# Twelve small tables copied into one and gathered jointly for the first two groups; dense features turned first; chunk 0 stored batch by batch

## The reference

```python
e = stack([tbl_f[ids[:, f]] for f in range(32)], axis=1)      # 512 x 32 x 64
# layer 0, then layer 1, with hidden = e at first
z = einsum('bhd,bfd->bhfd', hidden, e).reshape(B, -1, D)
y = relu(einsum('bcd,oc->bod', z, w) + b[None, :, None])      # 128 outputs
# layer 0: hidden = y[:, :64], direct = y[:, 64:]; layer 1: direct = y
z = concat(directs, axis=1).sum(-1)                           # 512 x 192
h = relu(concat([z, dense_ctx], 1) @ W_top1 + b_top1)
y = relu(h @ W_top2 + b_top2) @ W_top3
```

## Time and profile before

| | us |
|---|---|
| median of 3 runs | 1061.82 |
| lowest, highest | 1060.72, 1062.32 |
| the profiled execution | 1062.44 |
| its span | 1060.6 |

### The profile page before, as it was taken

How to read it: one execution, slowest core, us unless ns; L and a number is a source line. 1 busy time by engine, 2 the same in 40 slices (tenths; PEclk the granted TensorE clock), 3 DMA queues, 4 the chain that set the end, 5 groups by cost and what they waited for, 6 DMA issues and landing times.

```text
span 1060.6 us, 11306 instructions
## 1 busy us (share of the span) xinstructions
PE 1017.3 (96%) x3519; PEld 661.0 (62%) x3519; DVE 947.4 (89%) x777; ACT 770.0 (73%) x908; POOL 917.9 (87%) x310
## 2 busy tenths in 40 slices
PE   2399999999999999999999999999999999999999
PEld 1146566566666666666666666666766666666663
DVE  3089999999999999999999999999999999999991
ACT  5047666677878877877778777877787887788772
POOL 6528888799999999999999999999988989899880
PEclk9999999999999999999999999999999999999999
DMA  6498888878878877888778878887776776777630
GB/s 173 96 223 195 186 186 193 183 180 193 190 174 191 187 185 179 191 194 189 176 182 193 187 175 192 193 191 170 168 169 167 171 183 162 166 181 180 161 80 0
DMA packets 140638, 183.92 MB, mean 173 GB/s; under 512 B 55633, under 2 KB 56273, under 8 KB 140450
## 3 DMA queue, kind: packets, MB, share of 16 engines
q1 hardware_dynamic: 135986, 178.93, 72.0%
q0 software_dynamic: 4096, 4.20, 2.7%
q10 hardware_dynamic: 496, 0.06, 0.0%
HBM read 174.66 MB, written 8.39 MB: 173 GB/s over the span
## 4 chain that ended last, share of the span: by engine, by line
PE 64%; DVE 16%; issue 9%; ACT 4%; DMA 2%; ACTq 2%; SPq 1%; POOL 1%; POOLq 0%; DVEq 0%
PE py L723 28%; DVE zf L622 11%; PE py L743 11%; PE py L731 10%; PE py L732 10%; DVE zlB L642 2%; DMA xs<-x_dram 1%; ACTq L502 1%; DVE pzS L631 1%; ACT hid L470 1%; DVE zS L635 1%; ACT hid L469 1%; PE py L762 1%; POOL zl L380 1%; DMA xs<-in_L_rec_w 1%
## 5 line engine op out<-in xcount | busy, mean ns | idle before, releaser
L380 POOL TENSOR_TENSOR zl<-zf,zh 128x2048 fp32r<-128x2048 f32 x178 | 785.5, 4419 | 85.0 <-ACT zh L445 82.5
L622 DVE TENSOR_TENSOR zf<-xs,hid 128x2048 f32<-128x2048 f32 (+1 forms) x256 | 538.6, 2108 | 31.3 <-ACT hid L470 25.6
L723 PE MATMUL py<-zf,wf 128*128 128x512 f32 x944 | 426.9, 592 | 1.2 <-DVE zf L622 1.2
L445 ACT ACTIVATE zh<-zf 128x1536 fp32r<-128x1536 f32 (+1 forms) x184 | 338.2, 1838 | 94.5 <-DVE zf L622 90.5
L731 PE MATMUL py<-zh,wh 128*128 128x512 f32 x736 | 290.5, 395 | 1.5 <-ACT zh L445 1.1
L723 PEld LDWEIGHTS py<-zf,wf 128*128 128x128 f32 x944 | 178.4, 189 | 176.7 <-issue 161.5
L732 PE MATMUL py<-zh,wl 128*128 128x512 f32 x736 | 288.4, 392 | 0.0
L743 PE MATMUL py<-zl,wh 128*128 128x512 f32 x736 | 227.3, 431 | 1.4 <-POOL zl L380 1.4
L743 PEld LDWEIGHTS py<-zl,wh 128*128 128x128 f32 x736 | 138.7, 189 | 66.8 <-issue 36.8
L731 PEld LDWEIGHTS py<-zh,wh 128*128 128x128 f32 x736 | 138.4, 188 | 39.5 <-issue 8.5
L369 POOL DMA_INDIRECT emb<-in_tbl,idx x128 | 132.2, 1033 | 28.8 <-issue 22.6
(11 more groups left out here) (100 smaller groups left out, 608.8 us busy)
## 6 DMA issues: line engine op xcount, KB each, us to landing
xs<-x_dram SPq DMA_DIRECT2D x512, 256.0 KB
xs<-x_dram SPq DMA_DIRECT2D x504, 64.0 KB
x_dram<-emb SPq DMA_DIRECT2D x66, 64.0 KB, 5.6
x_dram<-emb SPq DMA_DIRECT2D x22, 96.0 KB
emb<-in_tbl,idx POOLq DMA_INDIRECT x128
x_dram<-emb SPq DMA_DIRECT2D x4, 384.0 KB
xs<-in_L_rec_w SPq DMA_DIRECT2D x2, 512.0 KB
xs<-in_L_rec_w SPq DMA_DIRECT2D x1, 1024.0 KB
```

Of the source, the lines that this page charges most:

```text
L380: pool.tensor_tensor(zl[:, q, first:T], zf[:, s, first:T], zh[:, q, first:T].bitcast(F32), ALU.subtract).then_inc(lo["P"], 1)
L445: act.activation(zh[:, q, first:T], zf[:, s, first:T], ACT.Copy).then_inc(hi, 1)
L622: dve.tensor_tensor(zf[:, slot(u), first:T], left[:, first:T], view(right, at, [[0, T - first], [1, N]]), ALU.mult).then_inc(mult, 1)
L723: mm = pe.matmul(y, wf[:, w, h], zf[:, s, h], start=first and h == first_tile, stop=ends and h == T - 1)
```

## The change

- `FIRST_BATCHES` is (fields 0-11), (12-16), (17-19), and, as the last, the twelve fields 20-31 (`REST`).
- SyncE copies tables 20 to 31 one after another into one DRAM table `table_joint`, with one transfer for each, after the weights; it loads the ids of the 8 samples of groups 0 and 1 for these fields into `ids_joint`, 96 partitions (12 fields x 8 samples) by 2. DVE builds the first row of each table in the joint one (memsets, times the identity, summed over columns, cast) and adds it to the ids.
- POOL, after the 20 single gathers, waits for the twelve copies and gathers group 0's and then group 1's 96 rows in one transfer each (`gather_joint`). The twelve fields of `REST` are gathered after these.
- SyncE puts group 0's 96 rows into `x32` with one transfer and stores them twice into `x_dram`, and group 1's twice. `load_xd(0)` waits for the stores of fields 0-19 and of joint group 0, `load_x0(1)` for joint group 1. The other 112 samples of `REST` are stored after `load_xe(0)`, and `load_x0(2)` waits for that.
- ScalarE issues eight `x32` transfers for the first batch, five for the second, two for the third; SyncE one for field 19.
- The dense features are loaded after the weights and turned by TensorE ahead of the weights; DVE copies them earlier. The top-layer weights are loaded at g == 50 (`load_top`) instead of at the start.
- One warm-up matmul fewer ahead of the spreading.

The diff, without its context lines:

```diff
@@ -55,12 +55,18 @@
-FIRST_BATCHES = [(0, 0, 12), (0, 12, 12), (0, 24, 5), (0, 29, 3)]
+JOINT = 20
+NJ = F - JOINT
+JOINT_GROUPS = 2
+FIRST_BATCHES = [(0, 0, 12), (0, 12, 5), (0, 17, 3), (0, JOINT, NJ)]
+REST = len(FIRST_BATCHES) - 1
-STORES = [sum(min(m, REPEATS) for b, _, m in BATCHES if b == c) for c in range(NC)]
+STORES = [sum(min(m, REPEATS) for n, (b, _, m) in enumerate(BATCHES) if b == c and n != REST) for c in range(NC)]
@@ -131,6 +137,13 @@
+        ids_joint = sb("ids_joint", [P, JOINT_GROUPS], I32)
+        idx_joint = sb("idx_joint", [P, JOINT_GROUPS], I32)
+        first_row = sb("first_row", [P, NS * NJ])
+        first_rows = sb("first_rows", [P, 1])
+        first_rows_int = sb("first_rows_int", [P, 1], I32)
+        emb_joint = sb("emb_joint", [P, JOINT_GROUPS, D])
@@ -204,7 +217,14 @@
-        ids_in, consts_in, top_in = sem("ids_in"), sem("consts_in"), sem("top_in")
+        offsets = [sum(t.shape[0] for t in tables[JOINT:JOINT + j]) for j in range(NJ + 1)]
+        table_joint = nc.dram_tensor("table_joint", [offsets[NJ], D], F32, kind="Internal")
+        ids_in, consts_in, top_in, dense_in = sem("ids_in"), sem("consts_in"), sem("top_in"), sem("dense_in")
+        ids_joint_in, tables_joined, rows_set, idx_joint_ready = sem("ids_joint_in"), sem("tables_joined"), sem("rows_set"), sem("idx_joint_ready")
+        joint_gathered = [sem("joint_gathered%d" % k) for k in range(JOINT_GROUPS)]
+        joint_stored = [sem("joint_stored%d" % k) for k in range(JOINT_GROUPS)]
+        rest_stored = sem("rest_stored")
@@ -254,25 +274,41 @@
+            sp.dma_start(dense[:], dense_ctx.rearrange("(c p) n -> p c n", p=P)).then_inc(dense_in, 16)
+            for k in range(JOINT_GROUPS):
+                first = ids[NS * k:NS * k + 1, JOINT:JOINT + 1]
+                sp.dma_start(ids_joint[0:NS * NJ, k:k + 1], bass.AP(tensor=first.tensor, offset=first.offset, ap=[[1, NJ], [F, NS], [1, 1]]),
+                             allow_slow_non_contiguous=True).then_inc(ids_joint_in, 16)
-            sp.dma_start(wt1a[H:P, :], W_top1[0:H, :]).then_inc(top_in, 16)
-            sp.dma_start(wt1b[:], W_top1[H:H + P, :]).then_inc(top_in, 16)
-            sp.dma_start(wt2[:], W_top2.rearrange("(k p) n -> p k n", p=P)).then_inc(top_in, 16)
-            sp.dma_start(wt3[:], W_top3.rearrange("(k p) n -> p (k n)", p=P), allow_slow_non_contiguous=True).then_inc(top_in, 16)
-            sp.dma_start(bt1[:], b_top1.rearrange("(k p) -> p k", p=P), allow_slow_non_contiguous=True).then_inc(top_in, 16)
-            sp.dma_start(bt2[:], b_top2.rearrange("(k p) -> p k", p=P), allow_slow_non_contiguous=True).then_inc(top_in, 16)
-            sp.dma_start(dense[:], dense_ctx.rearrange("(c p) n -> p c n", p=P)).then_inc(top_in, 16)
-            sp.wait_ge(cleared, 2)
-            sp.dma_start(wt1a[0:16, :], W_top1[H + P:H + P + 16, :]).then_inc(top_in, 16)
+            for j in range(NJ):
+                sp.dma_start(table_joint[offsets[j]:offsets[j + 1], :], tables[JOINT + j]).then_inc(tables_joined, 16)
+            def load_top():
+                sp.dma_start(wt1a[H:P, :], W_top1[0:H, :]).then_inc(top_in, 16)
+                sp.dma_start(wt1b[:], W_top1[H:H + P, :]).then_inc(top_in, 16)
+                sp.dma_start(wt2[:], W_top2.rearrange("(k p) n -> p k n", p=P)).then_inc(top_in, 16)
+                sp.dma_start(wt3[:], W_top3.rearrange("(k p) n -> p (k n)", p=P), allow_slow_non_contiguous=True).then_inc(top_in, 16)
+                sp.dma_start(bt1[:], b_top1.rearrange("(k p) -> p k", p=P), allow_slow_non_contiguous=True).then_inc(top_in, 16)
+                sp.dma_start(bt2[:], b_top2.rearrange("(k p) -> p k", p=P), allow_slow_non_contiguous=True).then_inc(top_in, 16)
+                sp.wait_ge(cleared, 2)
+                sp.dma_start(wt1a[0:16, :], W_top1[H + P:H + P + 16, :]).then_inc(top_in, 16)
-                if n == 3:
+                if n == REST:
+                    others = NS * JOINT_GROUPS
+                    for i in range(REPEATS):
+                        dst = x_dram[c, i * F + f:i * F + f + 1, D * others:D * others + 1]
+                        sp.dma_start(bass.AP(tensor=dst.tensor, offset=dst.offset, ap=[[D, P - others], [P * D, m], [1, D]]),
+                                     emb[others:P, c % 2, f:f + m, :]).then_inc(rest_stored, 16)
+                    return
+                if n == 2:
-                    load_x32(sp, 31, x32_last)
+                    load_x32(sp, f + m - 1, x32_last)
@@ -284,6 +320,13 @@
+            def store_joint(k):
+                sp.wait_ge(joint_gathered[k], 16)
+                if k == 0:
+                    sp.dma_start(x32[JOINT:F, :], emb_joint[0:NS * NJ, 0]).then_inc(x32_last, 16)
+                for i in range(REPEATS):
+                    sp.dma_start(x_dram[0, i * F + JOINT:i * F + F, N * k:N * k + N], emb_joint[0:NS * NJ, k]).then_inc(joint_stored[k], 16)
@@ -323,18 +366,26 @@
-            for n in range(len(FIRST_BATCHES)):
+            for n in range(REST):
+            store_joint(0)
+            store_joint(1)
+            sp.wait_ge(joint_stored[0], 16 * REPEATS)
+            sp.wait_ge(joint_stored[1], 16 * REPEATS)
+            store_batch(REST)
+            sp.wait_ge(rest_stored, 16 * REPEATS)
+                if g == 50:
+                    load_top()
@@ -363,6 +414,8 @@
+                    if c == 2:
+                        pool.wait_ge(rest_stored, 16 * REPEATS)
@@ -379,7 +432,19 @@
+            def gather_joint(k):
+                if k == 0:
+                    pool.wait_ge(idx_joint_ready, 1)
+                    pool.wait_ge(tables_joined, 16 * NJ)
+                pool.indirect_dma_start(
+                    out=emb_joint[0:NS * NJ, k, :], out_offset=None, in_=table_joint[:],
+                    in_offset=bass.IndirectOffsetOnAxis(ap=idx_joint[0:NS * NJ, k:k + 1], axis=0),
+                ).then_inc(joint_gathered[k], 16)
+                if n == REST:
+                    for k in range(JOINT_GROUPS):
+                        gather_joint(k)
@@ -495,17 +560,19 @@
-            for n in range(2):
-                _, f, m = FIRST_BATCHES[n]
-                act.wait_ge(gathered[n], gathered_count(n))
-                for b in range(NS):
-                    act.dma_start(x32[f:f + m, D * b:D * b + D], emb[b:b + 1, 0, f:f + m, :]).then_inc(x32_in, 16)
+            _, f, m = FIRST_BATCHES[0]
+            act.wait_ge(gathered[0], gathered_count(0))
+            for b in range(NS):
+                act.dma_start(x32[f:f + m, D * b:D * b + D], emb[b:b + 1, 0, f:f + m, :]).then_inc(x32_in, 16)
+            _, f, m = FIRST_BATCHES[1]
+            act.wait_ge(gathered[1], gathered_count(1))
+            for i in range(m):
+                load_x32(act, f + i, x32_in)
+            _, f, m = FIRST_BATCHES[2]
-            for f in range(24, 29):
-                load_x32(act, f, x32_in)
-            act.wait_ge(gathered[3], gathered_count(3))
-            for f in range(29, 31):
-                load_x32(act, f, x32_last)
+            for i in range(m - 1):
+                load_x32(act, f + i, x32_last)
@@ -537,6 +604,7 @@
+            act.wait_ge(top_in, 16 * 7)
@@ -565,6 +633,23 @@
+            for j in range(NJ):
+                dve.memset(first_row[:, NS * j:NS * j + NS], float(offsets[j])).then_inc(rows_set, 1)
+            dve.wait_ge(eye_in, 16)
+            dve.wait_ge(rows_set, NJ)
+            dve.tensor_tensor(first_row[0:NS * NJ], first_row[0:NS * NJ], ident[0:NS * NJ, 0:NS * NJ], ALU.mult).then_inc(rows_set, 1)
+            dve.wait_ge(rows_set, NJ + 1)
+            dve.tensor_reduce(first_rows[0:NS * NJ], first_row[0:NS * NJ], AX_X, ALU.add).then_inc(rows_set, 1)
+            dve.wait_ge(rows_set, NJ + 2)
+            dve.tensor_copy(first_rows_int[0:NS * NJ], first_rows[0:NS * NJ]).then_inc(rows_set, 1)
+            dve.wait_ge(rows_set, NJ + 3)
+            dve.wait_ge(ids_joint_in, 16 * JOINT_GROUPS)
+            dve.tensor_tensor(idx_joint[0:NS * NJ], ids_joint[0:NS * NJ], first_rows_int[0:NS * NJ].to_broadcast([NS * NJ, JOINT_GROUPS]),
+                              ALU.add).then_inc(idx_joint_ready, 1)
+            dve.wait_ge(dense_turned, 1)
+            dve.wait_ge(cleared, 2)
+            dve.tensor_copy(zd[0:16], px0[0:16]).then_inc(s_low, 1)
@@ -580,9 +665,6 @@
-            dve.wait_ge(dense_turned, 1)
-            dve.wait_ge(cleared, 2)
-            dve.tensor_copy(zd[0:16], px0[0:16]).then_inc(s_low, 1)
@@ -684,6 +766,10 @@
+            pe.wait_ge(dense_in, 16)
+            for c in range(NC):
+                tr = pe.transpose(px0[0:16, P * c:P * c + P], dense[:, c, :], ident[:])
+            tr.then_inc(dense_turned, 1)
@@ -693,10 +779,6 @@
-            pe.wait_ge(top_in, 16 * 8)
-            for c in range(NC):
-                tr = pe.transpose(px0[0:16, P * c:P * c + P], dense[:, c, :], ident[:])
-            tr.then_inc(dense_turned, 1)
@@ -777,9 +859,9 @@
-            warm_up(4, py1[:])
```

(6 more changed lines are left out.)

## The result

| | us | ratio to before, 95% interval |
|---|---|---|
| before, 20 runs beside it | 1061.76 | |
| after, 20 runs | 1064.44 | 1.0025, 1.0017 to 1.0032 |
| after again, in the fifth comparison below | 1065.42 | 1.0023, 1.0013 to 1.0034 |
| after again, in the sixth | 1057.63 | 0.9954, 0.994 to 0.9967 |

The change was slower by 0.25%, 2.7 us, where 7.3 less was forecast. The last row is no misprint: the same kernel was faster by 0.46% in another comparison, while the median of the kernel before lay between 1061.6 and 1062.7 in all. Most of this document is about finding why. The profiled execution of the result took 1063.91, with a span of 1062.1, against 1060.6.

What follows compares the result with a forecast made beforehand. TensorE bounds the long middle, a queue of 32 gathers the start. Spreading -14.1, tail +6.3, top weights +0.5 sum to -7.3 us: 1054.5 from 1061.82, its own range 1051.5 to 1057.5, whole range 1047.5 to 1062.0.

Steps and rivals of the forecast that it cites:

- Gain at the spreading: 14.1 us: At the start, the first real matmul (spreading of x32) would move from 48.76 to 34.7, a gain of 14.1 us.
- Copies in time: Before the joint gather: twelve table copies, 3.65 MB, would end at 20.6 to 28.9, before the gather's slot at 29.36.
- The rival that made it slower by waiting for the copies: At the start, POOL stands still until the copies end; at 108 GB/s +8 us, 1069.5; chance 0.14.
- the 10 of 16 engines: Table copies going row by row would use 10 of 16 DMA engines: 67 GB/s and 1085 or more.
- a copied byte count twice: In the table copies, each byte counting twice against HBM gives 179 GB/s, ending near 31, costing some 2 us.
- Crowding: Rival at the start: copies at 196 GB/s make the joint gather 3.1 late; 1057.6, up to 1061; chance 0.20.
- its second door: Crowding's other form at the start: batch 0's x32 transfers and stores stand behind the copies; no separate size.
- One of the signs of being wrong: At the start: ScalarE's small x32 transfers ending after SyncE's joint one would show the forecast wrong.
- Spreading to A(0): Start of chunk 0: steps after the spreading were taken to keep the old trace's distances, 11.06 us here.
- the 0.8 that I had put down as late: At the start of chunk 0, load_xd(0) would start 13.3 us earlier, 0.8 us late against compute.
- Tail of chunk 0: REST stores delay load_x0(2), landing at 64.3, holding up B(0) on TensorE: cost 6.3 us, range 3.5 to 8.
- Top weights at group 50: Seven transfers moved to group 50, issued in 4 us of SyncE idleness: cost 0.5 us, range 0 to 3.

Runs made afterwards that it cites:

- fifth comparison: Unedited rerun of the changed kernel (1065.42, ratio 1.0023), beside the kernel before (1061.48), the changed kernel with x32 read back (1064.84) and another version (1061.02).
- sixth: Unedited rerun of the changed kernel, 1057.63, ratio 0.9954, beside the unedited held version, 1058.76, ratio 0.9968.
- second comparison: Includes the changed kernel with POOL held before the twelve later gathers until the six spreading matmuls were counted: 1064.34.
- the fourth: Four kernels: four joint groups with POOL held (1058.20) or not (1060.74); kernel before with dense first and late top weights (1062.43), or a POOL pause (1065.60).
- held version: Changed kernel with four joint groups, POOL held before REST until the spreading was counted, REST stored at g == 1, seven warm-ups: 1058.20, ratio 0.9966.
- lean one: Held version with REST stored at the end of group 0, joint groups 2 and 3 stored later, top weights over seven groups: 1061.02, ratio 0.9983.

## Why the prediction was wrong

**The step that failed** is the unwritten one between "Gain at the spreading: 14.1 us" and the time at which the gain arrives. The sum took for granted that what follows the spreading moves with it, by the distances of the trace of before. In the result's comparison it didn't: from the spreading to DVE's first product it took 13.5 us (38.20 to 51.74) against 4.6. The spreading was 10.6 early and the first product 1.6; the second product (55.15 against about 54.0) and A(0) (62.08 against 59.82) were late. Before was profiled under the same condition, and its rows mostly hide it: the stores and transfers among the gathers were not urgent, and what was urgent came after the last gather of the burst (45.58). A distance read where nothing hurries can't show what a hand-over costs there. Two things did show it and were passed over: the four issues at 49.06 took 4.09 us, the same four at 849.02 took 1.85; and of the 4.6 us that were carried over from the old trace, ScalarE's copy alone stood 3.7 behind the start of the spreading, against 1.1 in the sixth comparison.

**What lies behind it is open.** Shown is: in four of six comparisons some 1.5 releases a microsecond are recorded while the gathers run and for 5 to 8 us after the last one begins, in all kernels; counts that TensorE raises in that stretch reach the others late, and SyncE's issues are slow; holding POOL ends it early (dense records from 35.75 and the first product at 41.89, second comparison); the two others have none of it. Not shown is what makes it: something of the chip's state, or the recording itself, which would be slowing what it records. The lost records speak for the second, as they go with the lateness comparison by comparison, but they can be its consequence as well, and every execution here was recorded, the timed ones at least by their span. It isn't the chip by its number, as the same number had both. So the kernel's worth on a machine is one of two, 1.0025 and 0.9954, and the runs don't say how often each.

**Point by point**, with the result's comparison first and the sixth second:

- *Copies in time.* Right in both. Their pieces ran from 9.2 to 21.5 and from 9.4 to 21.9, 12.3 us for 3.65 MB or 296 GB/s in the first, near the fast end of what I had drawn (11 to 19.4 us with the gathers beside). The rival that made it slower by waiting for the copies is out, and with it the 10 of 16 engines: the Trainium skill ("DMA: Bandwidth & Descriptors", "Why a DMA increments its semaphore by 16 and not by 1") gives 10 for 1250 rows, but the trace has each table as 16 pieces of 20,000 bytes (16,000 for 1000 rows), with up to 16 of them in flight at once. Nor did a copied byte count twice against the 358 GB/s that the Trainium skill gives in the section "Bandwidth" of that page: twice 296 would be 592.
- *Crowding.* This rival did occur, through its second door, batch 0 behind the copies. Its stores began at 22.40 and 22.80, against 20.55: the rows of its last gather were in at 21.5 and 21.8, against 20.2, behind the pieces of the copies. ScalarE's small transfers took 0.75 and 0.72 each, not 0.67, and in the result's run they also began 1.5 us later than in the sixth comparison (24.31 against 22.86), behind a ScalarE instruction that waited 1.73 us there. So the spreading began at 38.20 and 36.87, not at 34.7: 3.5 and 2.2 short. One of the signs of being wrong came with it: ScalarE's small transfers ended after the joint one (36.28 against 33.82, and 34.83 against 33.97), so ScalarE's chain set the spreading and not SyncE's.
- *Spreading to A(0).* 11.06 in the trace of before and in the forecast; 23.9, and 12.0. In the sixth `x0(1)` had to be waited for (3.30), the 0.8 that I had put down as late.
- *Tail of chunk 0.* SyncE waited for the `REST` stores in both, 6.1 and 5.1 us, and `x0(2)` was copied at 69.60 and at 63.07, forecast 64.3. In the first it hid behind the lateness: B(0) came 16.0 after A(0), as before (16.2). In the sixth TensorE reached B(0) at 66.80, 9.2 early (forecast 68.2, 7.8 early), and not after 6 us of idleness; but the loads behind `x0(2)` were late too, DVE waited 3.70 for them until 71.88, where I had looked only as far as B(0), and from the eighth of ScalarE's copies of `x0` on the lead is about 5.5. So the tail took 10.9 - 5.5 = 5.4 us of the lead at A(0), forecast 6.3. Size right, place half right.
- *Top weights at group 50.* Mis-sized: 0.5 forecast. In the sixth:

```profile
820.47 1.17 SPq L288 DMA_DIRECT2D wt1a<-in_W_top  x1
...
826.56 0.56 SPq L296 DMA_DIRECT2D wt1a<-in_W_top  x1
```

```profile
839.82 0.70 DVE L703 TENSOR_TENSOR pzB<-xs,px 128x512 f32<-128x512 f32 x1 [2.17 <-DMA xs<-x_dram]
```

The seven took 6.65 us to issue, not 4 (1.2 for some, where I took 0.57 from stores), and the new wait of DVE on DMA that was to be absent is 2.17 us, 1.84 in the result's profile. ScalarE's copies of `x0` are 4.9 us ahead of before's just ahead of the top weights and 2.6 ahead after them: 2.3 us, within the 0 to 3 that I had given it.

**The sum in the sixth comparison**, by the profiled spans: -14.1 + 2.2 (crowding) + 1.0 (`x0(1)`) + 5.4 + 2.3 = -3.2; the span is 1057.9 against 1060.6, -2.7, and the medians differ by 4.6. The sum leaves out that the lead of the copies falls from 5.5 to 4.9 ahead of the top weights, for which no cause was looked for. The profiled execution, 1059.69, was the slowest of the six. In the result's comparison the lead at A(0) is gone (+2.3), and the end is at +1.5 by span, 2.7 by the runs. So even without the late hand-over the gain was 4.6 us and not 7.3, 1057.6 against 1054.5: within the whole range, and 0.1 above the forecast's own (to 1057.5).

**Which version to use.** In the sixth comparison after and the held version are equal within their intervals. In the fifth the lean one, 0.9983, stands below after, 1.0023, and the intervals don't overlap. So four joint groups with the later gathers held cost nothing where counts are prompt, and the lean version, which has them too, saves some 4 us where they aren't. That isn't the hold's merit alone: lean differs from after by its joint groups, its warm-ups, the place of the `REST` stores and the spread-out top weights as well, and the hold by itself, in the second comparison, ran at 1064.34 in one execution, as after did in the first. Lean is the safer choice, though it was never run under prompt counts, and its own executions spread from 1056.92 to 1069.63.

## What to carry to other kernels

Work moved into a stretch in which a queue of indirect gathers runs brings its hand-overs between engines with it; their delay there can't be read off a profile in which nothing in that stretch was urgent, so price it by an experiment with one wait of the same kind. Time the changed kernel in more than one comparison when its gain hangs on such hand-overs: here one kernel was slower by 0.25% and faster by 0.46%, each with a narrow interval, and a different kernel in the other comparison would have got the credit. And follow a late load past the first user that it delays, to those issued behind it.

## What the runs showed of the hardware

- In four of six comparisons, while GpSimd issued one indirect gather every 1.25 us, TensorE's counts reached ScalarE 7 to 16 us after the matmuls where these fell into the burst of gathers (46.73 for 39.7 in after, 55.19 for 39.0 with x32 read back), and SyncE's issues were slow (four loads in 4.91 us, eight spare transfers in 7.24 to 11.18); both ended 5 to 8 us after the last gather began. In the sixth comparison the same kernel had the count 0.04 us after the matmul (38.01 for 37.97) and issued four loads in 2.06 us; the four kernels of the fourth had counts as prompt.
- In the same four comparisons most records of semaphore updates in that stretch are missing from the trace, though the updates took place: 38 of 192 for the table copies in after, 192 of 192 in the sixth comparison, with the waiting gather at 29.31 and 29.30.
- Copies of contiguous tables from DRAM to DRAM ran at 296 GB/s, a copied byte counted once, with nine gathers beside them; the rows of batch 0's last gather were in 1.3 and 1.6 us later (21.5 and 21.8 against 20.2), its stores began 1.9 and 2.3 us later.
- Of TensorE: in the result's run the granted clock was 0.50 (1.2 GHz) in the warm-ups from 31 to 35, after TensorE had idled from 19.1 to 31.06, 1.00 (2.4 GHz) from 37 to 38.2, and 0.50 again from 39.7 to 42, within the spreading (its first two records took 1.50 us instead of 1.02; 2.2 us of idleness lay ahead of it). With seven warm-ups it was 1.00 from 31 to 45, and nothing came earlier.
